# First attention of a two-layer block: two buffers for the weighed rows, the product that follows them taken later, and the output projection computed in two pieces of columns

## The reference, cut to what matters

```python
xn = _ln(x, g_attn, b_attn)
qkv = (xn @ qkv_w + qkv_b).reshape(b, s, 3, H, HD)
q, k, v = ...                                   # (b, 16, 256, 8) each
scores = jnp.einsum('bhqd,bhkd->bhqk', q, k) / np.sqrt(HD)
scores = jnp.where(causal, -jnp.inf, scores)
attn_w = jax.nn.softmax(scores, axis=-1)
attn = jnp.einsum('bhqk,bhkd->bhqd', attn_w, v)
attn = jnp.transpose(attn, (0, 2, 1, 3)).reshape(b, s, d)
attn = attn @ out_w + out_b
x = x + attn
```

## Time and profile before

| what | value |
|---|---|
| median of three runs | 1013.97 us |
| profiled execution, its own time | 1014.14 us |
| its span, first to last instruction | 1012.3 us |
| PE busy | 930.3 us, 92% |
| DVE busy | 616.3 us, 61% |
| ACT busy | 552.0 us, 55% |
| POOL busy | 460.2 us, 45% |
| mean granted clock of TensorE | 0.989 |

### The profile page before, as it was taken

One profiled execution on the slowest core, in us unless ns is written; L12 is line 12 of the kernel. 1 busy time (PEld: TensorE's weight loads), 2 busy tenths in 40 slices (PEclk: granted clock), 3 DMA queues, 4 the chain that ended last, 5 costly groups with the idle time before them and its releaser, 6 DMA issues.

```text
span 1012.3 us, 21410 instructions
## 1 busy us (share of the span) xinstructions
PE 930.3 (92%) x7335; PEld 590.9 (58%) x7335; DVE 616.3 (61%) x2028; ACT 552.0 (55%) x1077; POOL 460.2 (45%) x697
## 2 busy tenths in 40 slices
PE   8999999999989979999887998889997899999997
PEld 4566677777654223334533886456664444399994
DVE  4788888888815966863633544577873653344444
ACT  6536666667657554565511554557785622255551
POOL 1146776776642946630074454335543044323331
PEclk9999999999999999999998999999999999999999
DMA  6720000000010000040011224100000000121115
GB/s 207 245 79 13 13 8 13 13 8 13 13 60 35 0 1 1 0 167 0 1 51 49 79 78 154 50 2 1 2 2 1 1 29 30 37 57 49 49 31 177
DMA packets 38617, 45.95 MB, mean 45 GB/s; under 512 B 7872, under 2 KB 31936, under 8 KB 37648
## 3 DMA queue, kind: packets, MB, share of 16 engines
q1 hardware_dynamic: 34000, 35.26, 11.4%
q0 software_dynamic: 4512, 9.32, 2.8%
HBM read 31.32 MB, written 18.69 MB: 49 GB/s over the span
## 4 chain that ended last, share of the span: by engine, by line
PE 78%; DVE 7%; ACT 6%; issue 4%; another core or an unknown queue 1%; DMA 1%; POOL 1%; DVEq 0%; SPq 0%; POOLq 0%
PE PS L697 6%; PE PS L452 5%; PE PS L494 5%; PE PS L680 5%; PE PS L687 5%; PE PS L348 4%; PE PS L465 4%; PE PS L640 3%; PE PS L357 3%; PE PS L631 3%; PE PS L633 3%; PE PS L554 2%; PE PS L445 2%; PE PS L790 2%; PE PS L809 2%
## 5 line engine op out<-in xcount | busy, mean ns | idle before, releaser
L918 ACT ACTIVATE pw<-PS 128x384 f32<-128x384 f32 x256 | 111.6, 488 | 73.0 <-PE PS L474 71.4
L1607 POOL TENSOR_SCALAR_AFFINE_SELECT pw<-pw 128x256 f32<-128x256 f32 x256 | 103.7, 429 | 75.8 <-ACT pw L918 74.6
L1206 DVE CUSTOM_DVE_ANT_0 PS<-PS,above 128x256 f32<-128x256 f32 x256 | 114.1, 446 | 38.4 <-PE PS L445 36.2
L1673 POOL DMA_INDIRECT token_rows<-xnb,slot_in x77 | 73.9, 959 | 114.2 <-ACT xnb L1032 107.6
L1659 POOL TENSOR_TENSOR XS<-XS,N 128x512 f32<-128x512 f32 x64 | 81.1, 1288 | 55.7 <-DVE N L1280 35.0
L452 PE MATMUL PS<-kf,qm 32*128 32x256 f32 x512 | 103.2, 426 | 0.5 <-POOL qm L1616 0.5
L1459 DVE TENSOR_TENSOR rsb<-sqb,PS 128x256 f32<-128x256 f32 (+1 forms) x77 | 42.6, 553 | 93.6 <-PE PS L687 44.8
L1208 DVE CUSTOM_DVE_ANT_0 PS<-PS,above 128x128 f32<-128x128 f32 x256 | 84.7, 331 | 0.0
L1629 POOL TENSOR_SCALAR_AFFINE_SELECT pw<-pw 128x256 f32<-128x256 f32 x128 | 56.0, 472 | 59.6 <-ACT pw L1077 59.6
L1015 ACT ACTIVATE sqb<-PS 128x512 f32<-128x512 f32 x48 | 28.7, 597 | 99.4 <-PE PS L631 80.6
L1370 DVE TENSOR_TENSOR rsb<-sqb,PS 128x512 f32<-128x512 f32 x48 | 32.9, 688 | 78.5 <-PE PS L633 55.9
(11 more groups left out here) (212 smaller groups left out, 2336.2 us busy)
## 6 DMA issues: line engine op xcount, KB each, us to landing
sorted_rows<-empty_rows_dram SPq DMA_DIRECT2D x2, 2535.0 KB, 14.7
slot_in<-sorted_rows SPq DMA_DIRECT2D x77, 65.0 KB
N<-token_rows SPq DMA_DIRECT2D x16, 256.0 KB, 5.0
X<-xT_dram SPq DMA_DIRECT2D x8, 256.0 KB, 5.2
token_rows<-empty_rows_dram SPq DMA_DIRECT2D x1, 2048.0 KB, 24.4
ATT<-gate_dram SPq DMA_DIRECT2D x1, 2048.0 KB
XS<-down_dram SPq DMA_DIRECT2D x1, 2048.0 KB
H<-up_dram SPq DMA_DIRECT2D x1, 2048.0 KB
```

Of the source, the lines that this page charges most:

```text
L918: nc.scalar.activation(pw[:, w % 2, j + n, :], PS[:, A_PST + (2 * v + n) % 3, 0:3 * P], ACT.Exp).then_inc(a_p, 1)
L1206: nc.vector.tensor_tensor_reduce(x[:, 0:SEQ], x[:, 0:SEQ], above[:, :], 1.0, -3e38, ALU.add, ALU.max, mxs[:, t // 8 % 2, 1, j, g, 0:1])
L1607: m = nc.gpsimd.affine_select(x[:, :, SEQ * k:SEQ * k + P], x[:, :, SEQ * k:SEQ * k + P], [[0, 2], [1, P]], ALU.is_ge, 0.0, base=0, channe ...
L1673: nc.gpsimd.indirect_dma_start(token_rows[l][:, :], bass.IndirectOffsetOnAxis(slot_in[:, r, D:D + 1].bitcast(mybir.dt.int32), 0), slot_out ...
```

## The change

`av` becomes two buffers, one for even and one for odd batches, in chunks 0 and 1 of `sqb`. `keep_weighed(b)` waits for the `normalise` of b - 2 and no longer of b - 1. `normalise` goes from u = 3 to u = 5 for batches 0 to 12. For batch 13 it goes from step 131 to 130, and its `exp_sums` from step 130 to 128. The output projection of batches 0 to 12 is computed in two pieces: columns 0 to 159 at u = 7 as before, columns 160 to 255 two steps later, at u = 1, ahead of the transposes of the maxima. ACT adds the bias of the second piece behind its copy of the maxima. `a_att` now counts two per batch.

```diff
-        av, rec, ao = sqb[:, 0, :], rsb[:, 0, :], xnb[:, 0, :]
+        av = [sqb[:, (b + 1) % 2, :] for b in range(BATCH)]
+        rec, ao = rsb[:, 0, :], xnb[:, 0, :]
...
+        A_CUT = 160
...
-        NORM_STEPS = {8 * (b + 3) + 3 if b < BATCH - 2 else 8 * (b + 2) + 6: b for b in range(BATCH)}
+        NORM_STEPS = {8 * (b + 3) + (5 if b < BATCH - 3 else 2) if b < BATCH - 2 else 8 * (b + 2) + 6: b for b in range(BATCH)}
...
-        EXP_STEPS = {8 * (b + 3) + 2 if b < BATCH - 2 else 8 * (b + 2) + 5: b for b in range(BATCH)}
+        EXP_STEPS = {8 * (b + 3) + (2 if b < BATCH - 3 else 0) if b < BATCH - 2 else 8 * (b + 2) + 5: b for b in range(BATCH)}
...
             def project_v(b):
-                if b:
+                if b >= 4:
+                    pe.wait_ge(a_att, 2 * (b - 3))
+                elif b:
                     pe.wait_ge(a_m, b)
...
+            def out_columns(first, last):
+                for c in range(2):
+                    m = nc.tensor.matmul(PS[:, A_PSM, SEQ + first:SEQ + last], wout[:, c, :], ao[:, c * SEQ + first:c * SEQ + last],
+                                         start=(c == 0), stop=(c == 1))
+                return m
...
             def transpose_maxima(b):
                 pe.wait_ge(a_sp, b + 1)
                 if b >= 3:
-                    pe.wait_ge(a_att, b - 2)
+                    pe.wait_ge(a_att, 2 * (b - 3) + 1)
+                    out_columns(A_CUT, SEQ)
...
-                elif b == BATCH - 3:
-                    pe.wait_ge(a_m, BATCH)
                 else:
-                    pe.wait_ge(a_att, b)
-                for c in range(2):
...
+                    pe.wait_ge(a_att, 2 * b)
+                out_columns(0, A_CUT if b < BATCH - 3 else SEQ).then_inc(a_pj, 1)
...
                 nc.scalar.activation(mrow[:, b % 2, :], PS[:, A_PSM, 0:3 * P], ACT.Copy).then_inc(a_m, 1)
+                if b >= 3:
+                    add_bias(b - 3, A_CUT, SEQ).then_inc(a_att, 1)
...
             def keep_weighed(b):
                 act.wait_ge(a_av, 4 * b + 4)
-                if b:
-                    act.wait_ge(a_on, b)
-                nc.scalar.activation(av[:, :], PS[:, A_PSO, :], ACT.Copy).then_inc(a_cp, 1)
+                if b >= 2:
+                    act.wait_ge(a_on, b - 1)
+                nc.scalar.activation(av[b], PS[:, A_PSO, :], ACT.Copy).then_inc(a_cp, 1)
...
             def normalise(b):
                 dve.wait_ge(a_inv, 2 * b + 2)
-                if b:
+                if 1 <= b < BATCH - 2:
+                    dve.wait_ge(a_mt, b + 3)
+                elif b:
                     dve.wait_ge(a_pj, b)
-                nc.vector.tensor_tensor(ao[:, :], av[:, :], rec[:, :], ALU.mult).then_inc(a_on, 1)
+                nc.vector.tensor_tensor(ao[:, :], av[b], rec[:, :], ALU.mult).then_inc(a_on, 1)
```

More of the change, by code:

```diff
@@ L296, in _ @@
                 for j in range(4):
-                    sp.dma_start(rec[32 * j:32 * j + 16, :], av[32 * j + 16:32 * j + 32, :]).then_inc(a_moved[b % 2], 16)
+                    sp.dma_start(rec[32 * j:32 * j + 16, :], av[b][32 * j + 16:32 * j + 32, :]).then_inc(a_moved[b % 2], 16)
             sp.wait_ge(a_av, 4 * BATCH)
@@ L427, in out_project @@
                     pe.wait_ge(a_va, BATCH)
-                elif b == BATCH - 3:
-                    pe.wait_ge(a_m, BATCH)
-                else:
-                    pe.wait_ge(a_att, b)
-                for c in range(2):
-                    m = nc.tensor.matmul(PS[:, A_PSM, SEQ:2 * SEQ], wout[:, c, :], ao[:, c * SEQ:(c + 1) * SEQ],
-                                         start=(c == 0), stop=(c == 1))
-                m.then_inc(a_pj, 1)
+                else:
+                    pe.wait_ge(a_att, 2 * b)
+                out_columns(0, A_CUT if b < BATCH - 3 else SEQ).then_inc(a_pj, 1)
             def row_scores(t, n, low):
@@ L936, in exp_sums, with add_bias @@
                 nc.scalar.activation(rec[:, :], rec[:, :], ACT.Exp, scale=-1.0).then_inc(a_inv, 1)
[L938 to L941, removed]
+            def add_bias(b, first, last):
+                return nc.scalar.activation(ATT[:, b * SEQ + first:b * SEQ + last], PS[:, A_PSM, SEQ + first:SEQ + last],
+                                            ACT.Identity, bias=col(C_OUTB))
             for t in range(A_STEPS):
@@ L957, in _ @@
                 if t in OUT_STEPS:
-                    add_bias(OUT_STEPS[t])
+                    act.wait_ge(a_pj, OUT_STEPS[t] + 1)
+                    if OUT_STEPS[t] < BATCH - 3:
+                        add_bias(OUT_STEPS[t], 0, A_CUT).then_inc(a_att, 1)
+                    else:
+                        add_bias(OUT_STEPS[t], 0, SEQ).then_inc(a_att, 2)
             ln(LN_G1)
@@ L1237, in spread_sums @@
                     dve.wait_ge(a_on, b)
-                nc.vector.stream_shuffle(rec[:, :], av[:, :], [16 + p % 16 for p in range(32)]).then_inc(a_sh, 1)
+                nc.vector.stream_shuffle(rec[:, :], av[b], [16 + p % 16 for p in range(32)]).then_inc(a_sh, 1)
             def normalise(b):
                 dve.wait_ge(a_inv, 2 * b + 2)
-                if b:
+                if 1 <= b < BATCH - 2:
+                    dve.wait_ge(a_mt, b + 3)
+                elif b:
                     dve.wait_ge(a_pj, b)
-                nc.vector.tensor_tensor(ao[:, :], av[:, :], rec[:, :], ALU.mult).then_inc(a_on, 1)
+                nc.vector.tensor_tensor(ao[:, :], av[b], rec[:, :], ALU.mult).then_inc(a_on, 1)
             dve.wait_ge(va_ones, 6)
@@ L1618, in residual @@
             def residual(b):
-                pool.wait_ge(a_att, b + 1)
+                pool.wait_ge(a_att, 2 * (b + 1))
                 s = slice(b * SEQ, (b + 1) * SEQ)
```

## The result

The kernel after takes 1007.06 us in the median of 15 runs (1004.63 to 1012.08), the kernel before 1014.63 us in 15 runs (1012.39 to 1017.66). The ratio is 0.9927, 95% interval [0.9916, 0.9938]: faster by 0.7%, where I had forecast 1006.9 us. The profiled span fell from 1012.3 to 1005.3 us.

The account below looks back on a forecast made before the run. PE, busy 930.3 of 1012.3 us, was taken as the bound. 6.5 us from `normalise` plus 0.66 from the last batches made 7.2 us off 1014.14: 1006.9 us, own range 1005 to 1010, 8 in 10 within 1003.5 to 1012.5.

Parts of the forecast that it names:

- `normalise` out of u = 3: 6.5 us: DVE's stall of PE at step u = 5 goes, 0.50 us in each of batches 0 to 12.
- the idle stretch beside `project_qk`: DVE idles behind the maxima of u = 5, 0.61 to 0.74 us; `normalise` fits there but for some 0.15 us.
- Its overhang at nothing: The 0.15 us of `normalise` beyond DVE's idle time at u = 5 costs 0; upper bound 2 us.
- The 160 columns: nothing, except at step 127: Shorter projection at u = 7 saves 0.32 us of PE, hidden behind POOL's mask; only batch 12 gains 0.32 us.
- The wait of PE for the mask: At the end of u = 7, PE would wait longer for POOL's mask, about 0.45 us.
- The 96 columns at u = 1: nothing: The second projection piece holds PE about 0.54 us in its idle time behind the transposes; taken as 0, upper end 3.3 us.
- The narrow bias on ACT: nothing: The bias of 96 columns at u = 1 fits ACT's 0.44 us of idling; taken as 0, at most 0.8 us.
- `normalise` against the `cut`: At u = 5 POOL's `cut` beside `normalise` takes 0.46 us more, hidden by POOL's 1.19 us of idling.
- The late DMAs: nothing, with 0.6 us to spare: SP's four DMAs land at 173.8 us, ahead of the logarithm due at 174.4; taken as 0, bound 5 us.
- The last batches: Step 131 loses a 0.65 us wait, moved `exp_sums` adds 0.31 us, step 127 gains 0.32 us: net 0.66 us.

Follow-up runs that it names:

- experiment 5: Kernel after with `normalise` of batches 0 to 12 at u = 4, behind that step's maxima; one run, 1004.33 us beside 1014.16.
- experiment 6: Kernel before with only DVE's values of u = 4 moved behind that step's maxima; ratio 0.9966 to the kernel before.
- experiment 2: Kernel after with `normalise` back at u = 3, one `av` buffer and batch 13 as before, so only the projection is cut; ratio 0.9996 to the kernel before.
- norm_only: Kernel before with two `av` buffers and `normalise` of batches 0 to 12 at u = 5, projection whole, batch 13 as before; ratio 0.9971, median 1008.63 us.
- experiment 4: Kernel after with POOL's first mask ahead of the cut of u = 6 and the projection whole at u = 7; ratio 0.9948, median 1007.11 us.
- experiment 7: Kernel after with `normalise` of batches 0 to 12 at u = 6 instead of u = 5; one run, 1030.47 us beside 1014.16.
- mask_first: Kernel after with POOL's first masked quarter of the next batch ahead of the cut of u = 6, projection in two pieces; ratio 0.9879, median 999.98 us.
- experiment 8: The eight-DMA kernel: kernel after with each of the four DMAs of line 299 cut in two of 8 rows; one run, 1054.14 us beside 1014.16.
- experiment 9: Kernel before with `normalise` at u = 5 only and one `av` buffer; one run, 1044.56 us beside 1014.16.

## Why the prediction was right, step by step
- *`normalise` out of u = 3: 6.5 us.* Right in size: 12 steps u = 5 fell by 0.50 us, and step 125 of the last batch from 2.23 to 1.70. The place was argued wrongly. I took the idle stretch beside `project_qk` for the condition. Experiments 5 and 6 show that in batches with `project_qk` it is enough that `normalise` and the values do not run in a row. In the last batch, which lacks it, the parted pair still cost about 0.2 us wherever `normalise` stood (step 126 in experiment 5, step 125 in experiment 6, step 127 in the kernel after). So DVE needs the time that `project_qk` gives it, but `normalise` need not stand beside it.
- *Its overhang at nothing.* Right in 12 batches. In the last, which has no `project_qk`, DVE comes late to the maxima of step 126. Step 127 fell by 0.15 us only (1.98 to 1.83), where I had 0.32 and where the two pieces alone give 0.31 (experiment 2). With the projection whole it grew by 0.17 us, from 1.98 to 2.15 in norm_only: that is the overhang, paid once.
- *The 160 columns: nothing, except at step 127.* Right, shown by experiments 2 to 4. The wait of PE for the mask grew as said: 0.29 us between records, and with the 0.17 us by which I took a record to end late, 0.46 against the 0.45 I gave.
- *The 96 columns at u = 1: nothing.* Right except at step 129, where they cost 0.12 us by themselves (experiment 2). The product held PE for 0.53 us to the first transpose (0.54 estimated), and the next step began 1.80 us after the last, as before:

```profile
158.82 0.69 PE L415 MATMUL PS<-xnb,wout 128*128 128x96 f32 x4
159.35 0.33 PE L429 MATMUL PS<-identb,mxs 128*128 128x128 bf16 x3
159.63 0.34 PE L471 MATMUL PS<-mrow,selb 32*128 32x384 bf16 x2
```

- *The narrow bias on ACT: nothing.* Right: it takes 0.36 us, and 0.21 us of idle time remain ahead of the exponentials:

```profile
160.12 0.36 ACT L947 ACTIVATE ATT<-PS,cols 128x96 f32<-128x96 f32 x1
160.69 0.87 ACT L926 ACTIVATE pw<-PS 128x384 f32<-128x384 f32 x2 [0.21 <-PE PS L480]
```

- *`normalise` against the `cut`.* Right: 1.22 us, hidden.
- *The late DMAs: nothing, with 0.6 us to spare.* Right, and so was the margin. In the kernel after the logarithm starts 157.93 - 153.43 = 4.50 us after the first issue without waiting, and 3.8 us are needed in most batches (experiment 7): 0.7 us to spare.

```profile
153.43 2.40 SPq L299 DMA_DIRECT2D rsb<-sqb  x4
...
157.93 0.63 ACT L940 ACTIVATE rsb<-rsb 128x512 f32<-128x512 f32 x1
```

  What I left out is how much it varies. In mask_first 4.19 us are left, and three logarithms wait, 4.55, 4.69 and 4.98 us after a first issue. There the four issues took 3.15, 3.33 and 3.58 us instead of 2.40.
- *The last batches.* Step 131 gave 0.71 us (0.65 forecast), the moved `exp_sums` cost 0.23 us at step 129 (0.31; 0.24 in experiment 4, without the 96 columns), step 127 gave 0.15 (0.32). Together 0.63 us against 0.66.

The terms sum to 12 x 0.50 + 0.53 + 0.63 = 7.16 us, against the measured 7.21. That the whole came out within 0.2 us of the forecast is partly luck, since the rest of the program varies by more between runs: `normalise` alone gave 6.5 us in the stretch and 3.7 us in the medians.

## What to carry to other kernels
A small operation on a lightly loaded engine can cost the busy one time when it stands in a row with another ahead of the work that the busy one's buffers wait for; part the two before looking for a larger idle stretch. This worked in full where a longer product followed within two steps, and not quite in the batch without one. Comparing a batch that lacks an operation with one that has it, in one trace, prices both the operation and what would hold the step without it. Before work is taken off a step, look at which wait ends it: here the shorter projection was worth next to nothing until one statement on POOL was moved, and 3.3 us then. Before a loss is put down to a wait, look at the granted clock of the same stretch.

## What the runs showed of the hardware that I had not expected
- **A pause of TensorE can cost more than itself.** In the eight-DMA kernel PE stood idle for 1.57 us ahead of 171.59 us, and behind it the granted clock was 0.59 and then 0.65 of full speed, that is, partly the lower level of 1.2 GHz. The windows behind the pause (length, busy times with counts, then the granted clock):

```profile
172.00:174.00 2.00, 2.00 (x32) 0.99 (x24) 1.37 (x8) 1.72 (x5) 1.90 (x4) 0.59 0.00 0
174.00:176.50 2.50, 2.49 (x26) 2.02 (x23) 0.75 (x5) 0.72 (x3) 1.13 (x3) 0.65 0.00 0
176.50:180.00 3.50, 3.47 (x56) 2.72 (x56) 3.08 (x18) 2.35 (x6) 2.44 (x5) 1.00 0.03 7
```

  The pair of records that starts a step took 0.50 us there instead of 0.34 us. Experiments 7, 8 and 9 lost more than their waits sum to, and in their traces the granted clock is below 1.00 behind several such pauses. The longest stretches at 0.50 are 290 to 316 us in experiment 7, behind a pause of 1.31 us ahead of 287.34, and 310 to 338 us in experiment 8. But the pause ahead of 155.64 us in the eight-DMA kernel was again 1.57 us long, and behind it the clock stayed at 1.00. In norm_only the clock fell to 0.64 between 292 and 296 us, and PE reached the layer norm 10.3 us after the start of step 138, where it took 9.7 us before and after. The runs don't show what decides it, and this is left open.
- **Narrow activations hardly get cheaper.** The bias took 0.47 us for 256 columns, 0.40 for 160 and 0.36 for 96, so cutting it in two costs about 0.3 us of ACT.
- **Four DMAs issued in a row** took 3.8 us from the first issue to the logarithm that waited for the last in eight of 13 batches of experiment 7, which is three issues of 0.6 us and a landing of 2.0 us. In the other five it was 4.16 to 4.37 us where the four issues took 2.73 to 2.97 us instead of 2.40, and 4.67 and 4.73 us where they took 2.40. The slowest landing in that trace was 2.9 us.
